# One core, two transformer layers with a routed feed-forward: experts' slots sorted by weight, the one-hot matrices made apart, the first tokens split in halves, and layer 0's second row products moved ahead

## The chip, the core and the metric

The kernel runs on one core of one Trainium2 chip. The metric is device microseconds (us) of one execution, median over the runs shown. All times below are from one profiled execution of the kernel before unless a run is named.

## The reference

Four stages change x (8 sequences of 256 tokens, 256 features) by a residual: cross attention, a feed-forward that keeps only its largest activations, cross attention with rotation and mask, and a mixture of 16 experts with a shared expert beside them. The last one matters most here:

```python
scores = jax.nn.softmax(logits, axis=-1).transpose(0, 2, 1)
topk_w, topk_idx = jax.lax.top_k(scores, cap)            # cap = 32 tokens of each (sequence, expert)
x_tok = jnp.take_along_axis(hidden[:, None], topk_idx[..., None], axis=2)
g = jnp.einsum('becd,efd->becf', x_tok, Wg)
u = jnp.einsum('becd,efd->becf', x_tok, Wu)
h = gelu(g) * u
eo = jnp.einsum('becf,edf->becd', h, Wd) * topk_w[..., None]
flat = flat.at[flat_idx].add(eo.reshape(-1, d))          # back to the tokens' rows
out = flat + shared                                      # the shared expert runs on all tokens
```

The order of the 32 slots of one expert has no effect on the sum that comes back to a token.

## The kernel before

Every engine runs an instruction stream of its own in the order written, and semaphores tie them together. There is no scheduler: the order in the program is the order on the engine. x stays in SBUF (x_sb) for the whole run. The stages and their stretches of the span are: attention of layer 0 (to about 143 us, with the key products, row maxima, exponentials and divisions pipelined over the eight sequences), the activation products (to 214), three top-k searches and small products (to 352), attention of layer 1 (to 428), shared expert and routing (to 528), dispatch (to 557), experts (to 700), combination (to the end).

An f32 matrix product is either written as it is, which the trace shows as two MATMUL rows for each, or split: every operand is written as a high part in type f32r (an ACT copy that rounds) and a low part (the remainder, by DVE or POOL), and three products of such parts are summed. whi and wlo are weights in parts, thi and tlo the tokens of an expert, hhi and hlo the hidden values, nhi and nlo the normalised tokens.

**Attention of layer 0** (PE's `attend`, L1264; DVE's `attend_first`, L1894; ACT's `attend`, L804). In the turn of sequence n, PE makes the score products of n in four pairs of heads (`key_scores`), the query projection (`project_q`) and two products over all keys (`first_rows`, `second_rows`, whose maxima DVE takes at L1846) for sequence n+2, and the output projection of n-1 (`project_out`). DVE divides by the softmax's sum in `divide` (L1862 keeps that sum above zero), adds the projection to x and takes the statistics of the next norm (`stats_second`, with a copy at L1781).

**Shared expert and routing.** Sixteen halves (`shared_half`) take 24 split products of 128x256 each, and `down` another 24 after every second one. DVE's `route` steps lie between its part of these halves, and each step waits for the one before. Four rounds of MAX8 and MATCH_REPLACE8 (L2228, L2229) mark the 32 largest scores of each row of 256 tokens; a running sum gives every marked token its slot (posT after a transposition).

**Dispatch** (PE L1660, DVE L2259, ACT L1047, POOL L693). For each sequence DVE compares slot numbers with posT (L2247), which gives G, the one-hot matrix of tokens by slots. PE multiplies nhi and nlo by G: eight products of 512 columns, and the result, moved by ACT (L1053), is XT, the tokens of all experts. DVE multiplies G by the scores (L2267, GW), PE transposes that in eight pieces (L1682), and ACT moves it to GWT (L1059).

**Experts.** 16 units of gate and up products, GELU on ACT (L1008), products and parts on DVE, and down products. ACT moves each unit's output (L1069) and SP sends it in four DMAs (L502) to EO, which holds the slots by sequence.

**Combination** (`combine`, L1709). For each sequence, 8 unsplit products of 128x256 with GWT as the stationary operand sum the experts' outputs on each token. DVE adds the result to x (L2287), and SP writes it out (L512). `combine(0, range(3))` stands before the last unit's down products.

## Time and profile before

| | |
|---|---|
| median of 3 runs | 732.81 us (731.25, 732.81, 737.49) |
| the profiled execution | 733.08 us, its span 731.1 us |
| mean granted TensorE clock | 0.972 |
| PE busy | 655.3 us of the span (90%) |
| DVE busy | 452.5 us (62%) |
| ACT busy | 353.8 us (48%) |
| POOL busy | 238.4 us (33%) |

The span goes from the first to the last instruction. Busy time is summed over instructions of an engine, so it tells how much work an engine has and not whether anyone waited for it. A row of the timeline gives the start, the length, and in brackets the idle time before the instruction with the event that ended it. The granted clock is a share of 2.4 GHz; 0.50 is 1.2 GHz.

### The profile page before, as it was taken

The numbers are of one execution on the slowest core, as the hardware profiler recorded it, in microseconds if no ns is written. First come the engines' busy times: TensorE is split into PE (matmuls) and PEld (weight loads), VectorE is DVE, ScalarE is ACT, GpSimd is POOL, SyncE is SP. The second block draws the span as 40 slices with busy tenths as digits, with TensorE's granted clock in tenths as the row PEclk, the third lists the DMA queues.
The fourth block names the chain that finished last, engine by engine and source line by source line (L and its number), as shares of the span: only waits on it lengthen the run. The fifth ranks groups of instructions, "written<-read, shape, count | busy, mean of one in ns | idle before, by whom it ended". The sixth has DMA issues, their size and how long they took to land.

```text
span 731.1 us, 13206 instructions
## 1 busy us (share of the span) xinstructions
PE 655.3 (90%) x4816; PEld 532.6 (73%) x4816; DVE 452.5 (62%) x942; ACT 353.8 (48%) x781; POOL 238.4 (33%) x251
## 2 busy tenths in 40 slices
PE   5898999899978778776999989999888999999998
PEld 3666667688866555544566558999877999999996
DVE  3779887011027386767777536448896877777703
ACT  3267667566643133232667575232276555655400
POOL 6654522600000600047765212000144455555400
PEclk9999999999999989986999989999999999999999
DMA  7856650790000234015676633000002566666313
GB/s 262 270 167 152 196 139 23 299 387 15 0 0 1 98 124 113 1 39 126 150 150 122 157 46 136 38 2 1 1 1 87 188 206 205 204 204 205 110 30 115
DMA packets 61348, 87.17 MB, mean 119 GB/s; under 512 B 17257, under 2 KB 50665, under 8 KB 60265
## 3 DMA queue, kind: packets, MB, share of 16 engines
q1 hardware_dynamic: 60496, 85.90, 39.0%
q8 instruction: 32, 0.52, 0.3%
q10 hardware_dynamic: 800, 0.59, 0.3%
q14 instruction: 20, 0.16, 0.1%
HBM read 63.54 MB, written 18.73 MB: 113 GB/s over the span
## 4 chain that ended last, share of the span: by engine, by line
PE 73%; DVE 14%; issue 5%; ACT 3%; POOL 2%; DMA 2%; ACTq 0%; DVEq 0%; POOLq 0%
PE ps L1100 71%; DVE keep L2034 2%; DMA keep<-in_x 1%; PE ps L1106 1%; DVE keep L2045 1%; DVE keep L2042 1%; DVE keep L2027 1%; ACT vp L772 1%; DVE G L2247 1%; DVE mcol L1846 1%; DVE hhi_s L2174 1%; ACT keep L800 0%; DVE att L2172 0%; ACT ps L896 0%; DVE keep L2267 0%
## 5 line engine op out<-in xcount | busy, mean ns | idle before, releaser
L1100 PE MATMUL ps<-keep 128*128 128x120 bf16 (+7 forms) x473 | 60.5, 257 | 20.0 <-DVE keep L2034 14.8
L1100 PE MATMUL ps<-thi,whi 128*128 128x256 f32 x256 | 73.8, 288 | 3.7 <-POOL tlo L702 2.1
L1100 PE MATMUL ps<-thi,wlo 128*128 128x256 f32 x256 | 72.4, 283 | 0.0
L1100 PE MATMUL ps<-tlo,whi 128*128 128x256 f32 x256 | 72.1, 282 | 0.0
L1100 PEld LDWEIGHTS ps<-keep 128*128 128x128 bf16 (+1 forms) x473 | 34.1, 112 | 41.4 <-DVE keep L2034 26.4
L896 ACT ACTIVATE ps<-ps 128x256 f32<-128x256 f32 x128 | 47.6, 372 | 33.9 <-PE ps L1100 33.8
L1008 ACT ACTIVATE att<-ps 128x512 f32<-128x512 f32 x48 | 28.6, 595 | 65.6 <-PE ps L1100 65.4
L562 POOL TENSOR_TENSOR kbr<-khi,keep 128x616 fp32r<-128x616 f32 x32 | 39.7, 1263 | 61.3 <-PE ps L1100 59.0
L1100 PE MATMUL ps<-xhi,phi 128*128 128x512 f32 x128 | 50.9, 397 | 2.9 <-ACT ps L896 2.9
L1100 PEld LDWEIGHTS ps<-thi,whi 128*128 128x128 f32 x256 | 48.5, 190 | 5.8 <-issue 3.1
L1100 PE MATMUL ps<-xlo,phi 128*128 128x512 f32 x128 | 50.3, 393 | 0.0
L1100 PE MATMUL ps<-xhi,plo 128*128 128x512 f32 x128 | 50.3, 393 | 0.0
L1100 PEld LDWEIGHTS ps<-tlo,whi 128*128 128x128 f32 x256 | 48.8, 191 | 0.0
L1100 PEld LDWEIGHTS ps<-thi,wlo 128*128 128x128 f32 x256 | 48.5, 189 | 0.0
L1100 PE MATMUL ps<-kbr,qhi 128*128 128x154 f32 (+1 forms) x128 | 39.0, 416 | 10.0 <-ACT qhi L746 3.4
L2172 DVE TENSOR_TENSOR att<-att,ps 128x512 f32<-128x512 f32 x48 | 32.7, 681 | 23.3 <-ACT att L1008 20.6
L772 ACT ACTIVATE big<-ps 77x512 f32<-77x512 f32 x64 | 34.4, 589 | 23.6 <-PE ps L1100 23.3
L1100 PE MATMUL ps<-big,vp 77*32 77x256 f32 (+1 forms) x384 | 45.1, 383 | 0.5 <-issue 0.2
L1846 DVE TENSOR_REDUCE mcol<-ps 128x12 fp32r<-128x924 f32 x32 | 35.7, 1114 | 7.9 <-PE ps L1100 7.8
L772 ACT ACTIVATE vp<-ps 77x512 f32<-77x512 f32 x64 | 34.2, 584 | 12.6 <-PE ps L1100 12.1
L695 POOL TENSOR_TENSOR nlo<-big,nhi 128x512 fp32r<-128x512 f32 x8 | 12.5, 1566 | 83.9 <-ACT nhi L1035 83.9
L1100 PEld LDWEIGHTS ps<-kbr,qhi 128*128 128x128 f32 x128 | 25.8, 208 | 17.3 <-issue 7.9
(252 smaller groups left out, 1853.0 us busy)
## 6 DMA issues: line engine op xcount, KB each, us to landing
q_rows<-qhi SPq DMA_DIRECT2D x32, 256.0 KB, 2.7
big<-in_piw SPq DMA_DIRECT2D x4, 2048.0 KB, 13.4
qpair<-q_rows SPq DMA_DIRECT2D x8, 768.0 KB, 5.7
qhead<-q_rows SPq DMA_DIRECT2D x8, 768.0 KB, 7.5
q_rows<-qlo SPq DMA_DIRECT2D x16, 256.0 KB, 2.9
att<-in_wg SPq DMA_DIRECT2D x8, 512.0 KB, 3.9
att<-in_wu SPq DMA_DIRECT2D x8, 512.0 KB, 4.8
att<-in_wd SPq DMA_DIRECT2D x8, 512.0 KB, 5.6
```

The costliest lines, as they stand in the source:

```text
L562: ins = pool.tensor_tensor(kbr[n % 2][:, g], words(khi)[:, g, SK * b:SK * b + SK].unsqueeze(1).to_broadcast([P, HG, SK]), hmask.unsqueeze( ...
L695: pool.tensor_tensor(nlo[b % 3], xn_all[:, 2 * b:2 * b + 2, :], nhi[b % 3], ALU.subtract).then_inc(nlo_done, 1)
L772: act.activation(PT[n // B][0:SK, 2 * p:2 * p + 2, :], ps[0:SK, p % 2, :].rearrange("p (e q) -> p e q", e=2), ACT.Exp, scale=-0.25 if n < ...
L896: ins = act.activation(part, part, ACT.Gelu, accum_out=acts[:, bass.ds(ch * 8 + (2 * g + h), 1)])
L1008: act.activation(hgl[:, f, :], ps[:, 2 * f, :], ACT.Gelu).then_inc(gelu_done, 1)
L1100: return pe.matmul(out, lhsT, rhs, start=start, stop=stop, skip_group_check=True)
L1106: ins = pe.transpose(ps[:, bank, at:at + P], src[:, t, P * c:P * c + P], ident)
L1846: dve.tensor_reduce(heads[:, :, 0:6], ps[:, R_BANK:R_BANK + 2, 0:6 * SK].rearrange("p g (h k) -> p g h k", k=SK), AX, op, negate=True)
L2027: dve.scalar_tensor_tensor(out=levels, in0=digit[:, 1:RADIX].unsqueeze(2).to_broadcast([P, above0, 8]), scalar=float(RADIX ** (DIGITS - 1 ...
L2034: dve.tensor_tensor(reached[:, lo:hi, 8:P].rearrange("p c (j b) -> p c j b", b=8), chunked(keys)[:, lo:hi, :].unsqueeze(2) .to_broadcast([ ...
L2042: dve.scalar_tensor_tensor(out=mets[it % 2][:, 8:P], in0=ps[:, 7, 8:P], scalar=float(k), in1=level[:, 8:P], op0=ALU.is_ge, op1=ALU.mult).t ...
L2172: dve.tensor_tensor(hval, hgl[:, f, :], ps[:, 2 * f + 1, :], ALU.mult).then_inc(hval_done, 1)
```

## The change

**Attention of layer 0.** In PE's turn of a sequence `project_q` comes before the first pair of scores, `first_rows` and the output projection before the second pair, and `second_rows` before the third. ACT's `high_queries` and `normalise_second` move ahead likewise, and DVE's `stats_second` comes before the second maxima. In both layers the copy after BN_AGGR is gone (the result is written in place), and `divide` of layer 0 loses the step that keeps the sum above zero.

**Routing.** Each of the four rounds gets a MAX_INDEX. The 32 weights and 32 token numbers of each (sequence, expert) row stand sorted in sorted_w and token_f. SP writes token_f to memory and reads all of it back to each of the 128 partitions (`lists`, 128x4096). PE transposes both tables and turns them by eight small products into slot_token and slot_weight, a number for each slot on its partition.

**One-hot matrices.** G comes from comparing a sequence's list with the number of the partition's own token: TENSOR_SCALAR in place of TENSOR_TENSOR. GW, its transpositions and GWT are gone. Their place is taken by slot_rows, the one-hot matrix with slots on partitions, one DVE comparison of 128x1024 for each sequence: one in the dispatch, two after it, three between experts, two at the end. The score is applied where ACT moves an expert's output (two ACTIVATE of 128x256 with a scale in place of one of 128x512).

**First tokens.** The tokens of expert 0 are rounded in two halves as their columns arrive, and DVE takes their low part.

**Combination.** EO is split into eo_hi (ACT) and eo_lo (DVE), three groups of slots first and the last group when it has landed; slot_rows is exact in f32r. Each product becomes two, and none stands before the last down products. DVE's and the first of POOL's expert loops are unrolled.

```diff
         def attend(layer):                                   # PE
+                    if m < hi and layer == 0:
+                        project_q(m)
                     key_scores(n, (0, 1))
...
+                    if layer == 0 and m < hi:
+                        if m >= 5:
+                            pe.wait_ge(xlo_done, m - 4)
+                        first_rows(m)
+                        if n > lo:
+                            project_out(n - 1)
                     key_scores(n, (2, 3))
...
+                    if m < hi and layer == 0:
+                        second_rows(m)
                     key_scores(n, (4, 5))
...
-            for h in range(10, 13):
-                shared_half(h)
-            pe.wait_ge(rt_dve, 18)
+            shared_half(10)
+            shared_half(11)
+            pe.wait_ge(rt_dve, 19)
+            for j, rows in enumerate((sorted_w, token_f)):
+                ins = pe.transpose(ps[0:CAP, 7, P * j:P * j + P], rows, ident)
+            ins.then_inc(rt_pe, 1)
+            shared_half(12)
...
+            sp.wait_ge(rt_dve, 19)                           # SP
+            sp.dma_start(ld, token_f).then_inc(list_out, 16)
+            sp.wait_ge(list_out, 16)
+            sp.dma_start(lists.rearrange("p b n -> p (b n)"), ld.rearrange("r s -> (r s)").partition_broadcast(P)
+                         ).then_inc(list_in, 16)
...
             for j in range(CAP // 8):                        # DVE
-                route(dve.max(mx8, work))
-                route(dve.match_replace(work, mx8, work, -1.0))
+                best = sorted_w[:, 8 * j:8 * j + 8]
+                route(dve.max(best, work))
+                route(dve.max_index(token_u[:, 8 * j:8 * j + 8], best, work))
+                route(dve.match_replace(work, best, work, -1.0))
                 if j == 1:
                     shared_half(10)
+            route(dve.tensor_copy(token_f, token_u))
             shared_half(11)
...
-                    dve.tensor_tensor(G[b % 2][:, t].rearrange("p (e s) -> p e s", e=E),
-                                      iota.unsqueeze(1).to_broadcast([P, E, 32]),
-                                      posT[:, t, E * b:E * b + E].unsqueeze(2).to_broadcast([P, E, 32]), ALU.is_equal
+                    dve.tensor_scalar(G[b % 2][:, t], lists[:, b], own_token[:, t:t + 1], None, ALU.is_equal
                                       ).then_inc(g_done, 1)
...
+                if h == 13:
+                    dve.wait_ge(list_in, 16)
                     slots_one_hot(0)
...
             def combine(b, groups):                          # PE
...
-                        ins = mm(ps[:, (6 + b) % 8, D * t:D * t + D], GWT[:, b, g, P * t:P * t + P], EO[:, g, b, :],
-                                 g == 0 and t == 0, g == 3 and t == 1)
+                        rows = slot_rows[:, b, g, P * t:P * t + P]
+                        for j, part in enumerate((eo_hi[b // 3][:, b % 3, g, :], eo_lo[:, g, b, :])):
+                            ins = mm(ps[:, (6 + b) % 8, D * t:D * t + D], rows, part,
+                                     g == 0 and t == 0 and j == 0, g == 3 and t == 1 and j == 1)
...
+            def low_outputs(b, groups):                      # DVE
+                dve.wait_ge(eo_high, b + 1 if groups.start == 0 else B + b + 1)
+                dve.tensor_tensor(eo_lo[:, groups, b, :], EO[:, groups, b, :], words(eo_hi[b // 3])[:, b % 3, groups, :],
+                                  ALU.subtract).then_inc(eo_split, 1)
```

**PE, one turn of layer 0, before** (kbr with qhi are the row products of n+2, qpair with kpair the scores, keep with att the query projection, att with big the output projection, big with vp the values):

```order
L1100 MATMUL ps<-qpair_58,kpair_62 77x256 x4
L1100 MATMUL ps<-keep,att 128x256 x4
L1100 MATMUL ps<-qpair_58,kpair_62 77x256 x4
L1100 MATMUL ps<-kbr_50,qhi_52 128x462 x2
L1100 MATMUL ps<-kbr_50,qhi_52 128x154 x2
L1100 MATMUL ps<-qpair_58,kpair_62 77x256 x4
L1100 MATMUL ps<-att,big 128x256 x4
L1100 MATMUL ps<-kbr_50,qhi_52 128x462 x2
L1100 MATMUL ps<-kbr_50,qhi_52 128x154 x2
```

The same turn now:

```order
L1146 MATMUL ps<-keep,att 128x256 x4
L1146 MATMUL ps<-qpair_58,kpair_63 77x256 x4
L1146 MATMUL ps<-kbr_50,qhi_52 128x462 x2
L1146 MATMUL ps<-kbr_50,qhi_52 128x154 x2
L1146 MATMUL ps<-att,big 128x256 x4
L1146 MATMUL ps<-qpair_58,kpair_63 77x256 x4
L1146 MATMUL ps<-kbr_50,qhi_52 128x462 x2
L1146 MATMUL ps<-kbr_50,qhi_52 128x154 x2
L1146 MATMUL ps<-qpair_58,kpair_63 77x256 x4
```

Both row products now stand ahead of the third pair of scores, and the output projection stands between them.

**DVE, the last two rounds of the search, now** (L2214 to L2218 are the part of shared half 11):

```order
L2271 MAX keep<-keep 128x8
L2272 MAX_INDEX keep<-keep 128x8
L2273 MATCH_REPLACE keep<-keep 128x256
L2271 MAX keep<-keep 128x8
L2272 MAX_INDEX keep<-keep 128x8
L2273 MATCH_REPLACE keep<-keep 128x256
L2276 CAST keep<-keep 128x32
L2214 TENSOR_TENSOR att<-att,ps 128x512
L2216 CAST hhi_s<-att 128x512
L2218 TENSOR_TENSOR hlo_s<-att,hhi_s 128x512
```

Before, four instructions stood where the first six stand, and half 11 followed at once. The CAST at L2276 is the 19th `route` step, for which PE now waits behind its half 11.

**ACT, the end of the experts, now** (L1026 is GELU, L1088 the move of an expert's output):

```order
L1026 ACTIVATE att<-ps 128x512
L1102 ACTIVATE eo_hi_79<-big 128x768
L1026 ACTIVATE att<-ps 128x512
L1102 ACTIVATE eo_hi_79<-big 128x768 x2
L1088 ACTIVATE keep<-ps,keep 128x256 x2
L1102 ACTIVATE eo_hi_80<-big 128x768 x3
L1088 ACTIVATE keep<-ps,keep 128x256 x2
L1102 ACTIVATE eo_hi_81<-big 128x768 x2
L1102 ACTIVATE eo_hi_79<-big 128x256 x3
```

Before, only the two GELUs and two moves of an output stood here. The move of expert 14's output is now behind three high parts.

## Rows read from the trace of the kernel before

**Rows 1.** Windows: stretch, its us, busy us (instructions) by engine, PE clock, DMA.
```profile
44.00:143.00 99.00, 91.03 (x636) 66.06 (x628) 72.18 (x196) 65.44 (x164) 45.47 (x65) 1.00 0.53 155
...
528.00:557.45 29.45, 24.42 (x145) 20.16 (x145) 24.31 (x32) 21.03 (x32) 10.20 (x7) 1.00 0.00 1
557.45:568.10 10.65, 9.13 (x72) 8.72 (x72) 9.22 (x9) 5.96 (x9) 7.36 (x4) 1.00 0.42 148
568.10:700.00 131.90, 131.82 (x1071) 130.09 (x1072) 98.98 (x119) 71.62 (x98) 63.99 (x28) 1.00 0.56 184
```

**Rows 2.** Timeline of the end: start, us, engine, line, what.
```profile
697.06 2.75 PE L1100 MATMUL ps<-big,vp 128*128 128x256 f32 x12
...
702.53 25.20 PE L1100 MATMUL ps<-big,vp 128*128 128x256 f32 x116
702.73 0.60 ACT L1069 ACTIVATE keep<-ps 128x512 f32<-128x512 f32 x1 [4.87 <-PE ps L1100]
...
727.77 0.75 DVE L2287 SCALAR_TENSOR_TENSOR keep<-ps,keep 128x512 f32<-128x512 f32 x1 [2.70 <-PE ps L1100]
```

**Rows 3.** The DMAs of L502: length of an issue on SP, time to landing.
```profile
L502 SPq DMA_DIRECT2D big<-keep x64: 606/608/1169, 574.9 to 705.3; - x64
...
DMA to landing us min/median/max: 2.0/2.0/2.9
```

**Rows 4.** Groups by line and form: busy us, mean ns of one, idle before.
```profile
L1862 DVE TENSOR_SCALAR keep<-keep 128x16 f32<-128x16 f32 x16 | 3.4, 210 | 0.6
L2228 DVE MAX8 keep<-keep 128x8 f32<-128x256 f32 x4 | 1.7, 425 | 0.1
L2176 DVE TENSOR_TENSOR hlo_s<-att,hhi_s 128x512 fp32r<-128x512 f32 x16 | 11.1, 692 | 0.5
```

**Rows 5.** Timeline of layer 0, DVE and PE.
```profile
71.66 1.11 DVE L1846 TENSOR_REDUCE mcol<-ps 128x12 fp32r<-128x924 f32 x1
83.84 1.11 DVE L1846 TENSOR_REDUCE mcol<-ps 128x12 fp32r<-128x924 f32 x1
...
30.83 0.89 PE L1100 MATMUL ps<-qpair,kpair 98*77 98x256 f32 x4 [1.46 <-DMA qpair<-m_rows]
```

**Rows 6.** Timeline of the routing, DVE, ACT and PE.
```profile
505.15 0.41 DVE L2229 MATCH_REPLACE8 keep<-keep 128x256 f32<-128x256 f32 x1
519.53 1.28 DVE L2247 TENSOR_TENSOR G<-keep 128x512 fp32r<-128x512 f32 x2
...
505.19 0.60 ACT L1008 ACTIVATE att<-ps 128x512 f32<-128x512 f32 x1 [4.22 <-PE ps L1100]
...
508.73 0.38 PE L1100 MATMUL ps<-swhi,hhi_s 128*128 128x256 f32 x1 [0.71 <-DVE hlo_s L2176]
```

**Rows 7.** Timeline and windows around an earlier wait of PE.
```profile
253.22 0.69 PE L1494 MATMUL ps<-keep 128*128 128x128 f32 x2 [3.04 <-ACT keep L960]
...
253.00:254.00 1.00, 0.78 (x3) 0.78 (x4) 0.48 (x1) 0.22 (x2) 1.00 (x2) 0.50 1.07 459
```

**Rows 8.** DMAs by source: KB each, median us to landing.
```profile
big<-in_op SPq DMA_DIRECT2D x1, 2048.0 KB, 7.7
...
big<-in_piw SPq DMA_DIRECT2D x4, 2048.0 KB, 13.4
```

**Rows 9.** Timeline of the dispatch, DVE and PE.
```profile
540.15 2.38 DVE L2247 TENSOR_TENSOR G<-keep 128x512 fp32r<-128x512 f32 x2
...
543.65 2.37 DVE L2247 TENSOR_TENSOR G<-keep 128x512 fp32r<-128x512 f32 x2
...
542.58 0.50 PE L1100 MATMUL ps<-G,nhi 128*128 128x512 f32 x1 [0.52 <-DVE G L2247]
...
544.54 1.04 PE L1682 MATMUL ps<-keep 128*128 128x128 f32 x8
...
557.45 0.36 PE L1100 MATMUL ps<-thi,whi 128*128 128x256 f32 x1 [2.14 <-POOL tlo L702]
```

**Rows 10.** The chain that ended last, between shared expert and dispatch.
```profile
528.12 3.14 PE ps L1100 x24
```

More of the change, by code:

```diff
@@ L706, in low_parts @@
                                    ALU.subtract).then_inc(d_split, 1)
-            with pool.Fori(0, E // 4) as t:
+            for q in range(4):
+                low_parts(0, q, True)
+            with pool.Fori(1, E // 4) as t:
                 for q in range(4):
-                    low_parts(t, q)
+                    low_parts(t, q, False)
         @block.scalar
@@ L815, in attend @@
                         values_out(2, PV_BANK + 1)
+                    if n >= 2 and layer == 0:
+                        normalise_second(n - 2)
                     exponentials(n, (2, 3))
@@ L829, in attend @@
                         normalise(n + 4)
-                    if n - 2 >= lo:
+                    if n - 2 >= lo and layer == 1:
                         normalise_second(n - 2)
@@ L1051, in _ @@
                 for c in range(DC):
+                    if b == B - 1 and c > 0:
+                        round_first_tokens(c - 1)
                     act.wait_ge(disp_ps, DC * b + c + 1)
@@ L2279, in two_experts @@
                         gated(t * 2 + (B + s), s, f, (hhi_e, hlo_e), True)
-            with dve.Fori(0, E // 2 - 1) as t:
-                two_experts(t, False)
-            two_experts(E // 2 - 1, True)
+                        if last and s == 1:
+                            low_outputs(f, MOVED)
+                    if s == 0 and t in (2, 4, 6):
+                        rows_of_slots(t // 2 - 1)
+            for t in range(E // 2):
+                two_experts(t, t == E // 2 - 1)
+            for b in range(2, B):
+                if b in (3, 7):
+                    rows_of_slots(b)
+                low_outputs(b, MOVED)
+            for b in range(3):
+                low_outputs(b, LAST_GROUP)
             for b in range(B):
+                if b > 0 and b + 2 < B:
+                    low_outputs(b + 2, LAST_GROUP)
                 dve.wait_ge(comb_ps, b + 1)
```

230 lines of the change are left out of this document (123 added, 107 removed).

## The prediction

> **What bounds the kernel now.** I read the windows by stage first, then the timeline where PE is idle and at the end, then the groups by form for prices. The windows show which stages belong to PE: in the experts' stage it is busy 131.82 of 131.90 us, and 1071 matrix products there give 0.123 us each, the pitch of a split product of 256 columns [rows 1]. The combination is PE's too: 116 instructions of f32 take 25.20 us, or 0.217 us each [rows 2], and as a product is two such instructions, one product costs 0.434 us. The dispatch is not PE's. DVE starts the comparisons of a sequence at 540.15 and those of the next at 543.65, a period of 3.50 us, while PE's products for one sequence, from 542.58 to 544.54, take 1.96 us and its transpositions 1.04 us; PE then waits for G [rows 9]. Layer 0's attention is shared: PE is busy 91.03 of 99.00 us, DVE 72.18, and the maxima of one sequence start 12.18 us after those of the one before [rows 1, 5]. The top-k searches, layer 1 and the experts' loop keep their order of products.
>
> **Layer 0: 3 us less.** PE's idle time in the window is 7.97 us [rows 1], plus the 1.46 us at 30.83 in which it waits for a DMA [rows 5]; nothing in the edit removes PE work, so 9 us is the most it can give. The query projection now stands ahead of that DMA wait and fills most of it. Per sequence DVE loses two steps of 0.21 us [rows 4] and a small copy. Against that the third pair of scores now comes after both row products, so ACT's exponentials of the later pairs, the rounding of x and the maxima's way out all start later in the turn, and the next query projection stands right behind them. In my hand count of a turn the early ones, in which ACT also normalises, come out unchanged near 12 us, and the last ones shorter by 0.6 to 1 us. One us at the start, one in the late turns and one at the drain make 3. If the later exponentials stop PE instead, 2 us are lost in place. Ends: 9 less, 2 more.
>
> **Routing: 4 us more.** Before, the fourth MATCH_REPLACE8 ends at 505.56 [rows 6]. Four MAX_INDEX stand ahead of that end now. The trace has none; the nearest row is MAX8 over the same 256 columns, 0.425 us [rows 4], and with its load of values I take 0.5 us each, 2.0 in all, and 0.15 for the cast: token_f is ready at 507.7. PE ends half 11 just before ACT's GELU of it, 505.1 [rows 6], and now stands in front of the transpositions with half 12 behind them: 2.6 us idle. If MAX_INDEX were free it would be 0.6, at twice the price 4.6. Such a gap can also cost clock: after 3.04 us of idle time PE ran at 0.50 [rows 7], after 2.14 us at 1.00 [rows 9, 1]. 2.6 lies between and nearer the first, so I take a fall and an estimate of 1.6 us for it (a little over 3 us of dense work at half speed); its ends are 0 and 3. Back come the 0.71 us for which PE waited at 508.73 [rows 6], since half 11's parts are then ready, and eight small products in place of two transpositions take 0.5 more. 2.6 + 1.6 - 0.7 + 0.5 = 4.0; ends 0 and 8.
>
> The list has to be there when DVE comes to the first G, at 519.5 before [rows 6], so now 523.5. Writing token_f takes 2.0 to 2.9 us to landing [rows 3], and one read of 2048 KB alone took 7.7 us [rows 8]: 507.7 + 2.9 + 7.7 = 518.3, which is 5 us early. Behind this wait on DVE stand halves 14 and 15, for which PE waits. If the read takes 13.4 us as those of in_piw did [rows 8], the list lands at 524.0 and costs half a us. Price nothing; the cover is 5 us.
>
> **Dispatch: 10.4 us less.** Before, the shared expert's last down products end at 531.26 [rows 10] and the experts begin at 557.45 [rows 9]: 26.2 us. Now DVE has two one-source comparisons per sequence and no GW, PE no transpositions, ACT no move to GWT. PE's 1.96 us per sequence [rows 9] is then the longest: POOL's nlo is 10.20 us for seven, 1.46 each [rows 1], ACT has two moves of 0.60 and one rounding. The first of the seven left waits 0.9 us for the addition of the shared result (its banks are reused), seven times 1.96 are 13.7, and rounding, subtracting and signalling the last half of expert 0's tokens takes 1.2 us, against the 2.14 us PE waited for whole ones: 15.8 us.
>
> A pair of comparisons took 1.28 us undisturbed and 2.38 us next to POOL [rows 6, 9]. With the same 1.1 us added to two shorter steps (0.43 each, an estimate from MAX8 over half the columns and a cast's speed) G takes 1.95 us, just under PE. The Trainium skill (SBUF — State Buffer, "SBUF: two separate sides") says that a DVE instruction in a 2-port mode and one of GpSimd lock each other out for a whole instruction. By that rule the new comparisons could wait for all of an nlo, 1.46 us, and the term would be 8 us in place of 10.4, since each sequence then takes 2.3 us. Whether the new form is blocked so, no row shows. Ends: 8 and 12.
>
> **Start of the experts: 1 us more.** Behind expert 0's low parts DVE has two comparisons of 128x1024 (1.4 us each at most, twice the 0.69 us of 512 columns [rows 4]) ahead of the low weights of expert 1. PE already waited there. Of the 2.8 us I take 1, since the first GELU lies beside them; ends 0 and 3. The three comparisons between experts and the double ACTIVATE cost nothing: DVE is busy 98.98 and ACT 71.62 of 131.90 us [rows 1], and PE asks for the hidden values one down and one half later. Without that cover they would cost 4 us.
>
> **End: 10.6 us less.** From the end of expert 14's down products (697.06) to the end of the span it was 34.0 us [rows 2]. Now, in PE's order: ACT's move of output 14 stands behind three high parts and takes two instructions, and no combination lies between, so the last down products wait 0.9 us; they take 24 x 0.123 = 2.95; three groups of four sequences are 48 products, 5.9 us. By then the last output has been moved (0.7), sent by four issues of 0.61 and landed in 2.0 to 2.9 [rows 3]: 5.2 to 6.1 us after the down products, so it is just there, and its high and low parts follow at ACT's and DVE's pace. The four last groups take 4 x 0.49, and 0.4 for an addition of DVE between; four whole sequences 64 products, 7.9 us; the last addition and output 0.75 + 2.6 us as before [rows 2]. The sum is 0.9 + 2.95 + 5.9 + 2.0 + 0.4 + 7.9 + 3.35 = 23.4. DVE's own list from the same point is 7 low parts of about 0.95, two comparisons, 8 small low parts and 8 additions of 0.75, some 18.5 us against PE's 20.1 to the last product. Ends: 12.4, which is the pure difference of products (64 x 0.434 less 128 x 0.123 = 12.0, and the stall away), and 7 if DVE sets the pace.
>
> **Sum.** -3 + 4 - 10.4 + 1 - 10.6 = -19.0. The span becomes 712.1, the execution 733.08 - 19.0 = 714.1; the median lies 0.27 under the profiled execution, so 713.8.
>
> **Rivals.** (1) DVE or ACT sets the pace where I gave it to PE: at the end (7 in place of 10.6), and in the dispatch (8 in place of 10.4), and layer 0 gives nothing. That makes -10 to -13, some 721. For it: DVE has under 2 us of room at the end and almost none in the dispatch. Against it: DVE's rows there are the longest I could justify. 0.12. (2) No long wait in the routing and all of layer 0's idle time taken: -19 - 4 - 4, 706 or less. Four MAX_INDEX would have to be nearly free. 0.08. (3) Slower: the read of the list. All 128 partitions read the same 16 KB. If those reads queue up on one place in memory, DVE stands before the first G with halves 14 and 15 behind it and PE behind those. Each us past 523.5 costs one. The 19 us gained are used up when the list lands at 542.5, so when 2 MB take 32 us (66 GB/s); 2048 KB took 7.7 and 13.4 us, but from different addresses [rows 8]. At 50 GB/s it would take 42 us, land 29 us late and make 743. 0.04, three parts in four of it beyond that point. The Trainium skill (SBUF — State Buffer, "A bandwidth-pool intuition that's wrong") gives HBM about 22.5 GB/s for each of 32 ports; if one port served the list, 2 MB would take 93 us and the sum would pass 780. No row shows such a read. (4) The rest, 0.76, is the forecast.
>
> **Numbers.** 713.8 us. The range takes in rival 1 and most of 2: 706 to 722. About 1% (7 us) is what a measurement of this kernel can tell from no change. Faster by more: 0.95 (all but most of rival 3); within 1%: 0.02; slower: 0.03.
>
> **What would show it.** MAX_INDEX and its load at 0.5 us, PE idle for 2.6 us before the 128x32 transpositions with a granted clock of 0.50 behind, and the list landed 10 to 11 us after token_f; G of two TENSOR_SCALAR under 2 us and eight dispatch products starting every 1.96 us; the experts' first product 16 us after the shared down products; one idle time of about 0.9 us before the last down products; split combination products at a pitch of 0.123, and the last addition waiting for PE. If additions wait for DVE's low parts instead, rival 1 holds. The prediction fails if DVE waits for the list for more than a few us, or if a turn of layer 0 is longer than before.

## The result, and the profile after

The changed kernel takes 725.60 us (median of 4 runs, 724.64 to 727.37), beside 732.03 for the kernel before in the same session (730.36 to 737.49). The ratio is 0.9889 with a 95% interval of 0.9859 to 0.9918: faster, by about 1.1%. The forecast was 713.8 us, with a range of 706 to 722; the gain is real, but less than half of what was forecast. The profiled execution took 725.76 us, its span is 723.9 us (before 731.1), its mean granted clock 0.969.

| stretch (marks on PE) | before | after | difference | forecast |
|---|---|---|---|---|
| start to the third group of activation products | 143.74 | 143.23 | -0.5 | -3 |
| from there to the first product with ghi | 298.97 | 302.03 | +3.1 | 0 |
| to the shared expert's last down products | 85.41 | 89.24 | +3.8 | +4 |
| to the first expert product | 29.33 | 19.90 | -9.4 | -10.4 |
| to the second half of expert 1's gate products | 10.71 | 12.56 | +1.9 | +1 |
| to the end of expert 14's down products | 128.90 | 133.22 | +4.3 | 0 |
| to the end of the span | 34.04 | 23.72 | -10.3 | -10.6 |
| sum | 731.1 | 723.9 | -7.2 | -19.0 |

Four terms fit within 1 us: routing, dispatch, the experts' start and the end. Three do not: layer 0, the stretch that nothing was to move, and the experts. In the trace after, the stretches end at 143.23, 445.26, 534.50, 554.40, 566.96, 700.18 and 723.90. The rows of PE at two of these ends (554.40 and 566.96) and at its longer waits are below, with start, us, engine, line, what, and in brackets the idle time and what ended it:

```profile
510.42 0.61 PE L1699 MATMUL ps<-keep 128*32 128x128 f32 x2 [2.80 <-DVE keep L2276]
...
551.51 0.50 PE L1146 MATMUL ps<-G,nhi 128*128 128x512 f32 x1 [1.74 <-DVE G L2293]
...
554.40 0.35 PE L1146 MATMUL ps<-thi,whi 128*128 128x256 f32 x1 [0.77 <-ACT big L1077]
...
566.96 0.39 PE L1146 MATMUL ps<-thi,whi 128*128 128x256 f32 x1 [1.16 <-DVE hlo_e L2218]
...
609.44 0.38 PE L1146 MATMUL ps<-thi,whi 128*128 128x256 f32 x1 [0.48 <-DVE wlo L2234]
...
701.19 0.36 PE L1146 MATMUL ps<-whi,hhi_e 128*128 128x256 f32 x1 [1.02 <-ACT keep L1088]
```

The row at 554.40 answers to the last of [rows 9], at 557.45. At 562.67, ahead of expert 1, PE waited 1.78 us for its low weights (0.86 before). In the experts behind there are seven waits for wlo between 591 and 683, 0.40 to 0.82 us and 4.1 us together; before there was none from 568.16 to the end of expert 14's down products. The window answers to [rows 1] (stretch, its us, busy us of PE, PEld, DVE, ACT and POOL, PE clock, DMA):

```profile
566.96:700.18 133.22, 129.00 (x1056) 127.19 (x1056) 104.66 (x123) 75.84 (x114) 62.84 (x27) 1.00 0.54 180
```

The search answers to [rows 6] and [rows 4]: a MAX_INDEX shows as two instructions, and costs 0.51 us.

```profile
502.14 0.09 DVE L2272 MATCH_VALUE_LOAD keep<-keep 128x8 f32 x1
502.22 0.42 DVE L2272 FIND_INDEX8 keep<-keep 128x8 uint32<-128x256 f32 x1
```

In the dispatch, the rows of DVE and of GpSimd (POOL) after show why PE waited 1.74 us at 551.51. Two comparisons take 0.87 us with POOL idle, 1.36 us beside an nlo, and 3.46 us where POOL's low down weights of expert 0 follow an nlo:

```profile
546.16 1.36 DVE L2293 TENSOR_SCALAR G<-vp,keep 128x512 fp32r<-128x512 f32 x2 [0.47 <-PE ps L1146]
...
548.00 3.46 DVE L2293 TENSOR_SCALAR G<-vp,keep 128x512 fp32r<-128x512 f32 x2 [0.48 <-PE ps L1146]
```

```profile
545.53 1.30 POOL L708 TENSOR_TENSOR nlo<-big,nhi 128x512 fp32r<-128x512 f32 x1 [0.53 <-ACT nhi L1057]
...
548.63 2.54 POOL L719 TENSOR_TENSOR wlo<-att,whi 128x1024 fp32r<-128x1024 f32 x1
```

The end answers to [rows 2]: the last two additions wait 1.17 us for PE each, so PE sets the pace there, as forecast.

```profile
718.64 0.75 DVE L2352 SCALAR_TENSOR_TENSOR keep<-ps,keep 128x512 f32<-128x512 f32 x1 [1.17 <-PE ps L1146]
720.56 0.75 DVE L2352 SCALAR_TENSOR_TENSOR keep<-ps,keep 128x512 f32<-128x512 f32 x1 [1.17 <-PE ps L1146]
```

### The profile page after: what moved, and what is told of

It is laid out like the page before. It is cut to its first block, busy times and chain, and to the rows that moved or that the text cites. A ratio compares the mean times of both kernels' runs of the same rounds, so it can differ in the third digit from the quotient of the medians.

```text
span 723.9 us, 13037 instructions
## 1 busy us (share of the span) xinstructions
PE 638.5 (88%) x4768; PEld 517.6 (71%) x4768; DVE 455.3 (63%) x931; ACT 357.5 (49%) x806; POOL 233.8 (32%) x250
## 4 chain that ended last, share of the span: by engine, by line
PE 61%; DVE 17%; issue 8%; ACT 7%; DMA 3%; POOL 2%; SPq 1%; ACTq 0%; DVEq 0%; POOLq 0%
PE ps L1146 60%; DVE keep L2076 2%; DMA keep<-in_x 1%; DVE keep L2087 1%; ACT whi L1041 1%; SPq L515 1%; DVE att L2214 1%; DMA big<-in_wd 1%; DVE wlo L2234 1%; PE ps L1152 1%; DVE keep L2084 1%; DVE keep L2069 1%; ACT big L788 1%; ACT vp L788 1%; DVE hlo_e L2218 1%
## 5 line engine op out<-in xcount | busy, mean ns | idle before, releaser
L1146 PE MATMUL ps<-keep 128*128 128x120 bf16 (+8 forms) x489 | 60.6, 255 | 20.3 <-DVE keep L2076 15.2
L1146 PEld LDWEIGHTS ps<-keep 128*128 128x128 bf16 (+2 forms) x489 | 34.7, 112 | 41.8 <-DVE keep L2076 26.9
L1026 ACT ACTIVATE att<-ps 128x512 f32<-128x512 f32 x48 | 28.6, 596 | 68.7 <-PE ps L1146 68.5
L2214 DVE TENSOR_TENSOR att<-att,ps 128x512 f32<-128x512 f32 x48 | 32.6, 680 | 24.6 <-ACT att L1026 21.2
L1146 PE MATMUL ps<-kbr,qhi 128*128 128x154 f32 (+1 forms) x128 | 37.7, 405 | 10.3 <-ACT qhi L762 3.8
L1146 PE MATMUL ps<-xhi,swhi 128*128 128x256 f32 x128 | 37.8, 295 | 0.0
L708 POOL TENSOR_TENSOR nlo<-big,nhi 128x512 fp32r<-128x512 f32 x8 | 10.3, 1290 | 83.5 <-ACT nhi L1057 83.5
```

The lines of the kernel that those rows point to most:

```text
L708: pool.tensor_tensor(nlo[b % 3], xn_all[:, 2 * b:2 * b + 2, :], nhi[b % 3], ALU.subtract).then_inc(nlo_done, 1)
L1026: act.activation(hgl[:, f, :], ps[:, 2 * f, :], ACT.Gelu).then_inc(gelu_done, 1)
L1146: return pe.matmul(out, lhsT, rhs, start=start, stop=stop, skip_group_check=True)
L2214: dve.tensor_tensor(hval, hgl[:, f, :], ps[:, 2 * f + 1, :], ALU.mult).then_inc(hval_done, 1)
```

## The experiments

Every ratio is to the kernel before, run beside it. "First expert product to end" is 173.65 us before and 169.50 after. A single profile of this stretch is good to about half a us: two variants below that change nothing in it gave 169.53 and 169.06. The kernel before gave 175.03 in its second profile.

**The kernel before, once more** (no edit).

> The kernel before, unchanged, for a second profile. From the start of the third group of activation products (143.74) to the first product with ghi (442.71) the first profile took 298.97 us; the changed kernel, whose work there is the same but for small copies, 302.03, and two variants of it 302.11 and 300.16. Theory: these stages have places where the granted clock falls for a few us or does not, whatever the kernel, so this run comes out anywhere between 298.9 and 302.5. Rival: the changed kernel costs 3 us there by itself, and this run gives 299.0 within 0.3.

One run, 737.28 us, span 735.3. Windows of the middle, the first profile of before, the second, and the changed kernel:

```profile
143.74:442.71 298.97, 257.36 (x1934) 181.60 (x1935) 159.80 (x417) 142.83 (x397) 78.36 (x105) 0.94 0.36 97
```

```profile
144.25:445.52 301.27, 257.62 (x1935) 180.71 (x1935) 160.47 (x417) 143.08 (x397) 78.40 (x105) 0.94 0.36 96
```

```profile
143.23:445.26 302.03, 258.36 (x1934) 181.42 (x1935) 157.83 (x410) 143.10 (x397) 78.34 (x105) 0.93 0.36 96
```

The same program took 2.3 us more, and the twelve variants of the changed kernel below, all alike there, took 297.5 to 306.1. The 3.1 us are variation from run to run, not the change. Much of it is clock: PE's granted clock was 0.50 for 30.7 to 44.4 us of this stretch in the sixteen profiles, by the clock records of their traces, and in the main the more of it, the longer the stretch (297.5 and 298.7 us with 30.7, 306.1 with 44.4). Before had 37.5 us of it in both its profiles, so the 2.3 us between them are something else; the changed kernel had 41.0. One place is at 312: the clock after falls to 0.50 where it stayed at 1.00 before, behind the same 1.03 us of idle time.

```profile
313.00:314.00 1.00, 1.00 (x13) 0.39 (x8) 0.00 (x0) 0.00 (x0) 0.00 (x0) 0.50 0.00 0
```

```profile
313.00:314.00 1.00, 0.97 (x20) 0.32 (x12) 0.00 (x0) 0.00 (x0) 0.00 (x0) 1.00 0.00 0
```

The first of these rows is the changed kernel's, the second that of before.

**The attention layers' edits alone** (before, with the diff's edits of `attend`, `divide` and the norm's statistics and nothing else).

> The kernel before with only the edits of the two attention layers (order of layer 0's turn, no copy after BN_AGGR, two steps less in divide); routing, dispatch, experts and end as before. Theory A: the edit gives 0.5 us by the start of the activation products at 143 us, as in the changed kernel (143.23 against 143.74), and the 2.5 us that the changed kernel lost between 310 and 440 are clock falls whose place depends on small shifts of time: they come back in this run in some form, and the time is within 2 us of the kernel before (ratio 0.998 to 1.003). Rival B: the stretch from 310 to 440 is as before, and the time is 0.5 us less. Rival C, the forecast's term: 3 us less, ratio 0.996, had the changed kernel not lost it otherwise.

Ratio 1.0018 (0.9987 to 1.0049). The third group of activation products begins at 143.25, as in the changed kernel (143.23): the edit is worth 0.5 us there, and no gain shows in the time. The forecast's 3 us (rival C, 0.996) lie outside the interval. Theory A and rival B (0.9993) both lie inside, so the time does not tell them apart. The first wait for a DMA differs from run to run (5.75 us here, 5.76 before, 6.13 after). Less this wait, eight of nine profiles with the changed kernel's layer 0 have the mark at 137.0 to 137.3 (one at 139.1), and the two of before at 138.0 and 138.3: the gain is nearer 1 us than 0.5.

**The normalisation of the last two turns put back.**

```diff
-                    if n >= 2 and layer == 0:
+                    if 2 <= n < hi - 2 and layer == 0:
                         normalise_second(n - 2)
...
-                    if n - 2 >= lo and layer == 1:
+                    if n - 2 >= lo and (layer == 1 or n >= hi - 2):
```

> The changed kernel with ACT's second normalisation back behind the third pair of exponentials in the last two turns of layer 0 only. Theory: the change gained 1.9 us by the last full turn (91.95 against 93.86) and gave 1.4 of it back in the last two, because this normalisation (1.08 us) now stands ahead of exponentials for which PE's fourth pair of scores waits (0.53 us at 103.41 and at 112.74). Those two waits go, and the third group of activation products starts 0.9 to 1.1 us earlier than in the changed kernel (143.23, so 142.2), as a stretch from the span's start less the first DMA wait. Rival: the drain is PE's own length and nothing moves.

Ratio 0.9872 (0.9840 to 0.9903). In the changed kernel PE waited twice behind this normalisation, 0.53 us each, at 103.41 and at 112.74. The first of these rows:

```profile
103.41 0.95 PE L1146 MATMUL ps<-qpair,kpair 98*77 98x256 f32 x4 [0.53 <-ACT big L788]
```

Both waits are gone, and the mark is at 141.47, or 135.61 behind the first wait for a DMA (5.86), beside 137.10 (143.23 less 6.13): 1.5 us less, more than the 0.9 to 1.1 expected. The 1.9 us that I wrote were too much, though: they compare row products that the edit moves within the turn. By the first early activation product, whose place is unchanged, the change was 0.8 us ahead (100.86 against 101.66), and 0.5 at the mark. This version is level with it at the first (100.70), so all of its gain lies in the last two turns.

**Half 12 ahead of PE's wait for token_f.**

```diff
-            shared_half(10)
-            shared_half(11)
+            for h in range(10, 13):
+                shared_half(h)
             pe.wait_ge(rt_dve, 19)
```

> The changed kernel with PE's half 12 ahead of its wait for token_f (the 19th route step), and the copies behind it moved accordingly. Theory: PE's 2.80 us of idle time before the transpositions becomes 1.0 to 1.7 us (its down products of the half now wait for DVE's half 11 instead), so 1 to 1.8 us less, plus up to 1.5 us if the granted clock then stays at 1.00. Rival: DVE's search is on the path in any order and the time does not move (within 0.5 us of the changed kernel).

Ratio 0.9851 (0.9820 to 0.9881). PE waits 1.84 us in place of 2.80, and from the first product with ghi to the first expert product it takes 107.90 us, beside 109.14: 1.2 less. The wait is longer than the 1.0 to 1.7 us expected, and the clock still fell (0.50 from 512 to 513), so the up to 1.5 us more for a steady clock did not come.

**GpSimd later.**

```diff
+                else:
+                    pool.wait_ge(t_hi, 2)
                 pool.wait_ge(d_hi, x + 1)
```

> The changed kernel with one wait more: GpSimd starts the low part of expert 0's down weights only when the second half of expert 0's tokens is rounded, so no longer beside the last comparisons of the dispatch. Theory: the pair of comparisons of sequence 7 took 3.46 us because that 2.54 us subtraction held the port; it now takes 0.9 to 1.4 us, PE's wait of 1.74 us before the last dispatch products goes, and the experts begin 1.7 us earlier after the shared expert's last down products (17.5 becomes 15.8). Time 1 to 2 us under the changed kernel, ratio to before 0.986 to 0.988. Rival: the load of expert 2, which waits for that low part, leaves 4 to 5 us later (551.25 becomes 556) and the subtraction now lies beside the comparisons behind the dispatch; PE waits that much longer before the second and third expert, and the time stays at 0.989.

Ratio 0.9926 (0.9900 to 0.9953). The dispatch gained its 2 us (17.90 from the shared down products to the first expert product), and then PE waited 7.07 us at 563.74 for the low weights of expert 1. First expert product to end: 174.63. DVE and POOL of this run:

```profile
550.88 5.66 DVE L2311 TENSOR_TENSOR slot_rows<-keep 128x1024 fp32r<-128x1024 f32 x2
```

```profile
550.58 2.63 POOL L721 TENSOR_TENSOR wlo<-att,whi 128x1024 fp32r<-128x1024 f32 x1 [4.14 <-ACT thi L1052]
553.17 2.28 POOL L716 TENSOR_TENSOR tlo<-big,thi 128x512 fp32r<-128x512 f32 x1
```

Two comparisons that take 1.22 us each alone, about 2.3 us as a pair, took 5.66 beside two instructions of POOL. The rival had named this place; that PE would wait 7.07 us there in place of 1.78, it had not. The rows are the clue to the cause: the two engines took turns.

**One move in place of two** (the scores are left out).

```diff
-                for t in range(2):
-                    ins = act.activation(eo[s][:, t, :], ps[:, 4 + s, D * t:D * t + D], ACT.Copy,
-                                         scale=slot_weight[:, bass.ds(x + E * t, 1)])
+                act.activation(eo[s], ps[:, 4 + s, :].rearrange("p (t d) -> p t d", t=2), ACT.Copy
```

> The changed kernel with one ACTIVATE of 128x512 for each expert's output in place of two of 128x256 with a scale (0.60 us in place of 0.84); the scores are left out of the result, all else is unchanged. Theory: in the experts the loop PE down, ACT move, rounding of weights, DVE low weights, PE gate and up takes 9.0 us where PE has work for 8.86; before it took 8.7. With 0.24 us back, the seven waits for low weights (0.40 to 0.82 us, 4.1 us in all, between 591 and 683) fall to two or less and the time drops by 2.5 to 4 us, ratio 0.984 to 0.986. Rival: those waits follow from the arrival of the weights or from the comparisons between experts, they stay, and the time drops by less than 1 us.

Ratio 0.9863 (0.9828 to 0.9898). Four of the seven waits stay (0.69, 0.57, 0.68, 0.69); first expert product to end 167.54, 2.0 less, where 2.5 to 4 were expected. A part of the cause, and less than I said.

**Gate and up weights loaded early.**

```diff
-                    sp.wait_ge(gu_split, t * 8 + (2 * q + 4))
                     sp.wait_ge(d_split, t * 4 + (q + 2))
-                    load_expert(t * 4 + (q + 3), (q + 1) % 2)
+                    load_pieces(t * 4 + (q + 3), (q + 1) % 2, (2,))
+                    sp.wait_ge(gu_split, t * 8 + (2 * q + 6))
+                    load_pieces(t * 4 + (q + 4), q % 2, (0, 1))
```

> The changed kernel with each expert's gate and up weights loaded as soon as both their low parts are made (two thirds of the load, some 4 us earlier), and only the down weights after GpSimd's low part of them. Theory: the waits of ACT for weights (0.87, 1.92, 0.83 us) go, and with them the waits of PE that follow from them (618.87 and the like): 1 to 2 us less, ratio 0.985 to 0.988; the waits that come from the double move of an output (0.48 after every second expert) stay. Rival: weight arrival is the only cause, and all seven waits go: 4 us less, ratio 0.983. Other side: the four output DMAs now stand behind two weight loads and the landing of outputs is late; then the last down products wait longer and nothing is gained.

Ratio 0.9884 (0.9853 to 0.9915). In the experts ACT no longer waits for a DMA, and five waits of PE remain (2.9 us). First expert product to end 168.39, 1.1 less. Arrival is a part as well, and no more. The ratio is that of the changed kernel within its interval, so this reading rests on one profile.

**DVE and GpSimd apart at the start.** POOL makes expert 1's low tokens first and expert 0's low down weights behind DVE's low weights of expert 1; slot_rows of 4 and 5 move.

```diff
+            pool.wait_ge(t_hi, 3)
+            pool.tensor_tensor(tlo[1], XT[:, 1:2, :, :].rearrange("p o c t -> p (o c t)"), thi[1], ALU.subtract
+                               ).then_inc(t_split, 1)
+            pool.wait_ge(gu_split, 4)
```

> The changed kernel with DVE and GpSimd apart around the start of the experts: GpSimd makes the low tokens of expert 1 first and expert 0's low down weights only after DVE has made expert 1's low weights; slot_rows of sequence 4 moves into DVE's wait before the tokens of expert 0, that of sequence 5 between two experts. Theory: the pair of comparisons of sequence 7 takes 1.35 us (3.46 before), the experts begin 14.8 us after the shared down products (16.8), and without two comparisons of 128x1024 in its way DVE has expert 1's low weights early enough that PE waits under 2 us before experts 1 and 2 together (1.78 + 1.16 now, 7.07 in the version in which GpSimd only waited): 3 us less than the changed kernel, ratio 0.984 to 0.987. Rival: expert 2's weights, loaded only after GpSimd's low part, now come 8 us later and PE waits for them instead; no gain.

Ratio 0.9900 (0.9863 to 0.9936). The dispatch is 2 us shorter (17.88), but first expert product to end is 173.44, 3.9 more: PE waited 0.86, 2.37, 1.30 and 0.74 us in the first three experts. POOL's two subtractions in a row (563.83 to 568.7) held DVE's parts of the hidden values for 2.13 and 2.72 us. Weights that came late (the rival) joined in: DVE then waited 4.45 us for the next rounded ones.

**GpSimd in DVE's gap.** It waits for the last comparison of the dispatch; slot_rows of 5 stands behind the addition of the shared result, that of 4 between experts.

```diff
+                else:
+                    pool.wait_ge(g_done, 2 * B)
```

> The changed kernel with GpSimd's low down weights of expert 0 placed in the 2.4 us in which DVE waits for tokens (GpSimd waits for the last comparison of the dispatch), slot_rows of sequence 5 in DVE's wait behind the addition of the shared result (1.48 us), that of 4 between two experts. Theory: as both engines never run a two-operand pass at once, this is the one place where the 2.54 us subtraction is free: G of sequence 7 takes 1.35 us, first tokens are at most 0.3 us late, the experts' first products come 17.9 to 18.2 us after the shared down products begin (19.9 now), and PE's waits in the first two experts fall from 2.9 to under 2 us. In sum 2.5 to 3 us less than the changed kernel; ratio 0.984 to 0.987. Rival: the first tokens' low part waits for all of the subtraction and the 2 us come back there.

Ratio 0.9847 (0.9801 to 0.9894). 18.97 us to the first expert product, since the moved comparison now makes PE wait 0.79 us for G of sequence 2; the first two experts' waits are 1.57 us. First expert product to end 168.40, 1.1 less. In sum it is 2.0 us less than the changed kernel, where 2.5 to 3 were expected: the dispatch took 0.8 us more than its 17.9 to 18.2.

**Another order in the experts' loop.** ACT rounds down weights ahead of the output's move, which stands behind the next expert's first rounding; loads as in the early version, down weights ahead of the outputs' DMAs.

```diff
+                    if not (first and q < 2):
+                        expert_out(t * 4 + (q - 2), q % 2, None if first else t * 128 + 64 * ((q - 2) // 2))
                     gelu_half(u, 0)
```

> The changed kernel with another order in the experts' loop, and no work removed: ACT rounds the down weights right after the down products and moves the output (two ACTIVATE, 0.84 us) only behind the next expert's rounding of tokens and gate weights; gate and up weights are loaded when their low parts are made, down weights when GpSimd's low part is made, ahead of the outputs' DMAs. Theory: the loop from PE's down products over ACT, GpSimd and DVE to the next low weights gets 0.84 us shorter than its 9.0, so under PE's 8.86, and arrivals have 4 us more: the seven waits of 0.40 to 0.82 us (4.1 us) go but for one or two, 3 to 4 us less than the changed kernel, ratio 0.983 to 0.985. Rival: GpSimd's subtraction now starts with DVE's work and they hold each other up, so the waits stay at 0.5 us each.

Ratio 0.9863 (0.9830 to 0.9895). First expert product to end 168.28, 1.2 less where I expected 3 to 4. But the waits that are left (0.50 + 0.64, 0.58 + 0.57, 0.58 + 0.57) stand only behind the three comparisons between experts.

**All four together**, drain, half 12, GpSimd in the gap and the loop's order.

> All of these in one: drain_norm, half12_first, pool_fits and paced. Theory: the parts add up, 1.0 + 1.2 + 2.5 + 3.5 = 8 us less than the changed kernel: from the first product with ghi to the end 250.5 us (258.7 in the changed kernel), time about 718 us, ratio 0.976 to 0.980. Rival: the experts' stage has one pace for all (DVE beside GpSimd), and an earlier start only makes longer waits, as in start_cleared; then 3 us less at most, ratio 0.984.

Ratio 0.9771 (0.9729 to 0.9812), 718.37 us. The mark of layer 0 is 1.8 us earlier than in the changed kernel (141.41), the first product with ghi to the first expert product takes 105.45 (109.14), first expert product to end 167.20 (169.50): 7.8 us, the 8 expected. (The stretch that the expectation puts at 258.7 us was 278.6 in the changed kernel and is 272.7 here.) DVE and POOL at one of its four comparisons:

```profile
630.57 1.22 DVE L2329 TENSOR_TENSOR slot_rows<-keep 128x1024 fp32r<-128x1024 f32 x1
...
632.13 3.00 DVE L2254 TENSOR_TENSOR wlo<-att,whi 128x1024 fp32r<-128x1024 f32 x1 [0.35 <-ACT whi L1056]
```

```profile
630.71 3.33 POOL L734 TENSOR_TENSOR wlo<-big,whi 128x1024 fp32r<-128x1024 f32 x1 [4.00 <-ACT whi L1056]
```

DVE's comparison makes POOL's subtraction 0.9 us longer, and that makes DVE's next one 3.00 us in place of 1.22. As I read it, one comparison of 1.22 us is paid twice.

**GpSimd's work given to DVE**, on top of the last. `low_parts` of POOL is gone; DVE gets

```diff
+            def low_down(x):
+                dve.wait_ge(d_hi, x + 1)
+                dve.tensor_tensor(wlo[x % 2][:, PIECES[2]], raw[x % 2][:, PIECES[2]], whi[x % 2][:, PIECES[2]],
+                                  ALU.subtract).then_inc(d_split, 1)
```

and the like for tokens, behind its first low weights and its second half of hidden values.

> combo with all of GpSimd's work in the experts' stage given to DVE (low tokens 128x512, low down weights 128x1024 for each expert); GpSimd does nothing from the dispatch's end on. Theory (one port): DVE and GpSimd never run such passes at once, so what counts for an expert is the sum of both. It was 6.04 us of DVE (two wlo of 1.22, two times 0.68 + 0.43 + 0.69) and 3.7 of GpSimd, 9.7 against PE's 8.86. On DVE alone GpSimd's two cost 1.22 + 0.69, and the sum is 7.95. PE's waits in the experts (5.2 us in combo) shrink to the price of the four comparisons beyond the room left, 4 x 0.3 us, so the stretch from the first expert product to the end falls from 167.2 to 163 us, ratio 0.971 to 0.974. Rival (busy shares, as the forecast read them): DVE at 88% and in order makes PE wait where GpSimd worked beside it; 2 to 6 us more than combo.

Ratio 0.9680 (0.9638 to 0.9722), 710.44 us, the best of all. First expert product to end 161.09. This is 6.1 us less than with all four edits, where 4.2 were expected: PE does not wait once between 553 and 683, so the four comparisons cost nothing either.

```profile
553.00:679.00 126.00, 126.00 (x1050) 125.92 (x1051) 114.25 (x151) 76.04 (x115) 0.00 (x0) 1.00 0.59 192
```

DVE is busier than ever (114.25 of 126.00) and PE does not wait for it. None of its low weights of 128x1024 took over 1.23 us, where up to 3.08 were seen with all four edits. The rival of busy shares is wrong in its sign.

**A fifth comparison between experts**, that of sequence 7, on top of the four together.

```diff
-                    if s == 0 and t in (1, 2, 4, 6):
-                        rows_of_slots(t // 2 - 1 if t > 1 else 4)
+                    if s == 0 and t in (1, 2, 4, 5, 6):
+                        rows_of_slots({1: 4, 2: 0, 4: 1, 5: 7, 6: 2}[t])
```

> combo with a fifth comparison of 128x1024 between experts (that of sequence 7, taken from the end, where PE sets the pace). Theory (one port): each comparison there costs PE about 1.15 us in two waits, as the four of combo show (0.51 + 0.56, 0.59 + 0.57, 0.59 + 0.57, and 0.50 + 0.64 in paced), though DVE is busy for three quarters of the stage; a fifth adds a fifth pair of waits at once and 1.15 us to the stretch from the first expert product to the end (167.2, so 168.3). Rival (cover, as forecast): the fifth lies in DVE's idle time and costs nothing; 167.2 or, with the work gone at the end, less.

Ratio 0.9756 (0.9721 to 0.9792). First expert product to end 167.68, 0.5 more than the version of four. The theory's 1.15 is out; from the rival's nothing a single profile can't tell 0.5. PE's waits grew by 0.2 us only, of which the fifth's own was 0.25; the next comparison's were 0.50 + 0.58. A comparison has no fixed price here; that it depends on what POOL does at that moment and on the room around it is my reading, which no run isolates.

**The same one edit on the changed kernel itself** (POOL's `low_parts` moved to DVE, nothing else).

> The changed kernel with only this edit: GpSimd's work in the experts' stage is given to DVE, the low down weights of expert 0 in DVE's wait before the first tokens. All else, the two slot_rows at the experts' start, the three between experts, the double move and the loads, as in the change. Theory (one port): this alone takes back what the changed kernel lost in the experts. G of sequence 7 takes 0.9 us (shared down products to first expert product 18.0 us, 19.9 now), the seven waits of 4.1 us fall under 1 us, the waits of the first two experts (2.9) under 2.5; from the first expert product to the end 165.0 us (169.5 now). Time 6 us less than the changed kernel, ratio 0.979 to 0.982. Rival (move and arrival): the waits come from ACT's longer move and from the weights, which are untouched; then they stay and only the dispatch's 2 us come, ratio 0.986.

Ratio 0.9788 (0.9754 to 0.9822), 718.27 us. G of sequence 7 took 1.37 us, the shared down products to the first expert product 17.91, first expert product to end 164.33. PE's waits from 591 to 683 are three: 0.67, 0.29 and 0.42. The double move, the comparisons and the loads are as in the change. The stretches and the time came as the theory said, or better. Two numbers did not: G took 1.37 us where 0.9 was expected, as an nlo still lies beside it, and the three waits make 1.4 us where under 1 was expected. No cast or subtraction of DVE in the experts is lengthened any more. From the first expert product to the end of expert 14's down products before took 139.6 us, the changed kernel 145.8 and this one 140.6, so 5.2 of the 6.2 us lost there came back with this one edit. The waits blamed on moves and arrivals were mostly consequences of the two engines taking turns; that the cause of the turns is one port is not seen in a trace.

That comparisons between experts cost what they do was measured only by adding one. A version of the changed kernel without its three was put on record too (theory: PE's seven waits stay, as ACT's move is the cause; rival: the waits behind the three comparisons go, 1.5 to 3 us less), but it gave no result.

## Why the forecast was wrong

- **Layer 0, -3, measured -0.5.** The step that failed is "One us at the start, one in the late turns and one at the drain". Start and late full turns together gave 0.8 us (at the first early activation product) where I counted 2; the last two turns gave nothing and took 0.3 back. Less the first wait for a DMA it is 1.2 and 0.9 us. ACT's second normalisation, which the forecast gave no price, stands ahead of exponentials for which PE waits there (0.53 us twice); putting it back in the last two turns alone gave 1.5 us. What kept the start and the late turns under their 2 us is open.
- **The middle at 0, measured +3.1.** The sum was not wrong here: the same program varied by 2.3 us between its two profiles, and the variants with the same work by 8.6. Without the middle the change is worth 10.3 us by the profiles; the ratio says 8.1 (0.0111 x 732), with 6.0 to 10.3 as its interval.
- **Routing, +4, measured +3.8.** The parts came near: 0.51 us for a MAX_INDEX, 2.80 us of idle time (2.6 forecast), and a clock of 0.50 from 511 to 513.4, which cost 1.3 us (1.6 forecast). The list was read in 8.4 us, landed at 520.2 and was wanted at 525.9; the rival of one slow place in memory is out.
- **Dispatch, -10.4, measured -9.4.** The pace was PE's, at 1.82 us for a sequence (1.96 forecast), so seven of them gained 1 us more than forecast. The 1.74 us of the last wait went against it. I had looked at nlo beside the comparisons and not at POOL's next instruction, which in the change no longer waits for tokens. The forecast also misread nlo: of the seven POOL instructions of [rows 1] only five are nlo, at 1.66 to 1.82 us beside DVE; two earlier ones alone took 1.29 and 1.27, so the lengthening could be seen before. The rule of the Trainium skill (SBUF — State Buffer, "SBUF: two separate sides") that was weighed there, one waits for the other's whole instruction, agrees with the last pair of comparisons, which ended at 551.46 with POOL at 551.17. The other pairs began when an nlo was half done, and their 0.87 us grew by 0.5 only.
- **Start of the experts, +1, measured +1.9,** within its bounds. The two comparisons took 3.46 us beside POOL's low tokens in place of the 2.8 counted: the same collision.
- **Experts, 0, measured +4.3: the step that made most of the miss.** "The three comparisons between experts and the double ACTIVATE cost nothing: DVE is busy 98.98 and ACT 71.62 of 131.90 us" took the room of each engine from its own busy time. But DVE and POOL share their room: 98.98 and 63.99 us add up to 163 of 131.90, some of it waiting for each other. Without waiting an expert needs 6.04 us of DVE and 3.7 of POOL against PE's 8.64 (72 products at the pitch of 0.120 that the version on DVE alone shows); of DVE's work in the experts, only what reads PSUM kept its length beside POOL (0.67 to 0.69 us in every row), and it is 1.36 of the 6.04. The kernel before stood on the edge already: between 570 and 690 its products start 0.12 us apart but for 24 gaps of up to 0.29, which make 2.2 us and don't show in PE's busy 131.82 of 131.90. Its lengths told of it as well. POOL's low tokens took 2.28 to 2.30 us in 14 of 16 experts and 1.27 where alone; DVE's low weights took 1.22 alone and up to 2.49. That the price "without that cover", 4 us, is near the measured 4.3 is luck: with the comparisons and the double ACTIVATE kept and only POOL's work moved, 1.4 us of waits were left.
- **End, -10.6, measured -10.3.** The wait before the last down products was 1.02 us (0.9 forecast), and PE set the pace.

Two rows of the kernel before that show the sharing: they overlap, and alone they took 1.22 and 1.27 us.

```profile
577.26 2.08 DVE L2192 TENSOR_TENSOR wlo<-big,whi 128x1024 fp32r<-128x1024 f32 x1 [2.22 <-ACT whi L1023]
```

```profile
578.20 2.29 POOL L702 TENSOR_TENSOR tlo<-big,thi 128x512 fp32r<-128x512 f32 x1
```

Rival 1 (DVE or ACT sets the pace, 721, given 0.12) was nearest to the time, in part by luck. Its nothing for layer 0 was near, but its 7 for the end and 8 for the dispatch were measured at 10.3 and 9.4. What made most of the miss, DVE and POOL taking turns in the experts, was not among the rivals.

The Trainium skill (Perfetto Trace Analysis, "Optimizing Scalar/DVE Operations") says that GpSimd and DVE share a read port and that handing work from one to the other might not help. These runs agree in that the two engines took turns, and go further: handing the work from GpSimd to DVE helped, by 6.1 us of the experts and the end in one version (167.20 to 161.09) and by 5.2 in the other (169.50 to 164.33), since DVE needs 1.22 us for the 128x1024 subtraction and POOL 2.4.

## What to carry to other kernels

Where DVE and GpSimd both work from SBUF, read an instruction's length beside the other engine against its length alone, and if they differ as here (1.22 and up to 3.0 us), add the two engines' work before calling either a cover. If the sum is near the pace of the engine that bounds, try giving all of it to the faster one of the two. And take a second profile of the kernel before: what differs between two of the same program is the least that a difference between two programs can mean.

## What the runs showed of the hardware

A DVE subtraction of 128x512 took 0.69 us alone and up to 2.84 us beside a GpSimd one; a GpSimd subtraction of 128x512 took 1.28 us alone and 2.3 us beside DVE's. DVE's 128x512 operation that reads PSUM took 0.67 to 0.69 us with GpSimd busy or not. Restarting after a wait in the experts cost PE some 0.1 us more: the first pitch is 0.19 to 0.23 us in place of 0.12. A read of one 16 KB table to all 128 partitions (2 MB) took 8.4 us, 0.9 us longer than one from 2 MB of distinct data (7.5).
